# Gate rows of a mixture-of-experts layer spread over the partitions by DMA instead of by matmul

## The reference, cut to what matters

```
x = x + attention(ln_over_channels(x))        # per image, 256 tokens, one head
t = tokens of x                               # 1024 x 64
xt = ln(t)
probs = softmax(xt @ Wr + br)                 # 8 experts
top_p, top_idx = top_k(probs, 2)
weights = top_p / sum(top_p)                  # the two gates of a token
xn = ln(xt)
y[e] = gelu((xn * ln_g[e] + ln_b[e]) @ W1[e] + b1[e]) @ W2[e] + b2[e]     # 64 -> 256 -> 64
out = t + weights[0] * y[top_idx[0]] + weights[1] * y[top_idx[1]]
```

## Time and profile before

| | us |
|---|---|
| median of 3 runs | 68.73 (68.43 to 68.88) |
| time of the profiled execution | 68.35 |
| its span, first to last instruction | 66.6 |
| TensorE matmul busy | 60.2 (90% of the span) |
| VectorE busy | 38.2 (57%) |
| ScalarE busy | 33.9 (51%) |
| GpSimd busy | 27.6 (41%) |

### The profile page before, as it was taken

One profiled execution on the slowest core, in us unless ns is written; L12 is line 12 of the kernel. 1 busy time (PEld: TensorE's weight loads), 2 busy tenths in 40 slices (PEclk: granted clock), 3 DMA queues, 4 the chain that ended last, 5 costly groups with the idle time before them and its releaser, 6 DMA issues.

```text
span 66.6 us, 1224 instructions
## 1 busy us (share of the span) xinstructions
PE 60.2 (90%) x364; PEld 32.9 (49%) x364; DVE 38.2 (57%) x164; ACT 33.9 (51%) x78; POOL 27.6 (41%) x53
## 2 busy tenths in 40 slices
PE   2998799799799999999998799999999999999940
PEld 0315366588356687752765434435152644353630
DVE  2368699279995997931099924807040924049640
ACT  5301356832379995397479991770724392700000
POOL 5766880004599982360798000433443000705200
PEclk9999999999999999999999999999999999999999
DMA  0343478620000000000000000000000000000311
GB/s 0 96 94 57 152 167 253 262 110 5 0 0 0 15 0 0 0 0 0 5 0 0 10 0 0 0 0 0 0 0 0 0 0 0 0 0 0 89 40 43
DMA packets 2959, 2.33 MB, mean 35 GB/s; under 512 B 1924, under 2 KB 2568, under 8 KB 2952
## 3 DMA queue, kind: packets, MB, share of 16 engines
q1 hardware_dynamic: 2632, 2.21, 11.6%
q10 hardware_dynamic: 320, 0.03, 0.4%
HBM read 1.98 MB, written 0.26 MB: 34 GB/s over the span
## 4 chain that ended last, share of the span: by engine, by line
PE 62%; DVE 22%; issue 4%; DMA 4%; SPq 3%; ACT 2%; DVEq 0%
PE banks L927 22%; PE banks L891 21%; PE banks L848 4%; DMA X<-in_x_dram 4%; DVE nmax L519 3%; PE banks L911 3%; PE banks L833 3%; DVE KS L513 2%; DVE X L505 2%; PE banks L870 2%; SPq L256 2%; PE banks L944 2%; ACT PR L388 2%; DVE T L537 1%; DVE X L569 1%
## 5 line engine op out<-in xcount | busy, mean ns | idle before, releaser
L424 ACT ACTIVATE H<-banks,PF 128x512 f32<-128x512 f32 x32 | 20.4, 686 | 11.2 <-PE banks L891 10.8
L891 PE MATMUL banks<-XE,W1F 64*128 64x256 f32 x128 | 18.2, 402 | 0.2 <-ACT H L424 0.2
L927 PE MATMUL banks<-H,W2F 128*64 128x512 f32 x64 | 15.4, 603 | 0.0
L327 POOL TENSOR_TENSOR acc<-acc,gated 128x512 f32<-128x512 f32 x5 | 6.4, 1276 | 19.2 <-DVE gated L664 19.2
L891 PEld LDWEIGHTS banks<-XE,W1F 64*128 64x128 f32 x128 | 11.1, 186 | 6.0 <-issue 4.9
L648 DVE COPY GS<-banks 128x512 f32<-128x512 f32 x8 | 5.5, 685 | 7.1 <-PE banks L911 7.1
L308 POOL TENSOR_SCALAR XE<-XF,PF,LB 128x256 f32<-128x256 f32 x15 | 8.2, 563 | 2.5 <-ACT XF L405 2.5
L789 PE MATMUL banks<-zeros 128*128 128x512 f16 x23 | 8.0, 467 | 1.3 <-POOL zeros L330 1.3
L664 DVE SCALAR_TENSOR_TENSOR gated<-banks,B2T,GS 128x512 f32<-128x512 f32 (+1 forms) x7 | 4.6, 673 | 7.0 <-PE banks L927 6.8
L292 POOL TENSOR_TENSOR rs<-base,half 128x4 f32<-128x4 f32 x4 | 4.1, 1016 | 9.8 <-DVE base L562 9.8
L927 PEld LDWEIGHTS banks<-H,W2F 128*64 128x64 f32 x64 | 4.0, 136 | 6.7 <-issue 6.6
(11 more groups left out here) (87 smaller groups left out, 71.9 us busy)
## 6 DMA issues: line engine op xcount, KB each, us to landing
W1F<-in_w_dram SPq DMA_DIRECT2D x1, 768.0 KB, 6.0
W2F<-in_w_dram SPq DMA_DIRECT2D x1, 512.0 KB, 5.5
W1F<-in_w_dram SPq DMA_DIRECT2D x1, 256.0 KB, 3.2
out_dram<-res SPq DMA_DIRECT2D x4, 64.0 KB, 1.8
X<-in_x_dram SPq DMA_DIRECT2D x2, 64.0 KB, 1.9
X<-in_x_dram SPq DMA_DIRECT2D x1, 128.0 KB, 2.4
WQK<-in_attn_w_dram ACTq DMA_DIRECT2D x2, 16.0 KB, 2.1
WQK<-in_attn_w_dram SPq DMA_DIRECT2D x2, 8.0 KB, 2.0
```

The lines of the kernel that those rows point to most:

```text
L327: nc.gpsimd.tensor_tensor(acc[h][:, :], acc[h][:, :], gated[s % 2][:, :], ALU.add)\
L424: nc.scalar.activation(H[:, r, :].rearrange("p (t n) -> p t n", t=PT), ps_z[g // J % 2][:, :, PIX * j:PIX * j + PIX], ACT.Gelu, bias=PF[:, ...
L891: nc.tensor.matmul(ps_z[q % 2][:, k, PIX * j:PIX * j + PIX], W1F[rows, e, j, :], XE[h][rows, e, :], start=True, stop=True).then_inc(z_read ...
L927: mm = nc.tensor.matmul(ps_y[s % 2][C * k:C * k + C, :], W2F[:, u, :], H[:, (2 * J * s + J * k + j) % RING, :], start=(j == 0), stop=(j == ...
```

## The change

The gates are no longer cut into fp16 parts, no longer scaled, and no longer spread by TensorE. `turn_gates(h)` transposes the fp32 `gate[h]` directly, 4 matmuls with the 128 x 8 gate as the weights and the fp32 identity as the moving operand, into 8 partitions. ScalarE copies that to `gateT[h]`, 8 rows of 512 fp32 values. SyncE writes it to a DRAM scratch `gates_kept[h]` (16 KB), waits for that to land, and reads each of the 8 rows back into 64 partitions by a DMA with a broadcast source: 2 DMAs of 128 KB for each step s, into a tile `GS[s]` of its own. `weigh(s)` waits for `gates_in[s]`. Stages 11 and 12 of the route, `spread`, `keep_gates`, `select_rows`, the clearing of `gcut` and the fp16 identity go. The order on TensorE and VectorE is written anew around the gap, `fold_sum` and `finish(0)` stand one step earlier, and `add_up(6)` is cut into two pieces of 256 columns.

```diff
+        gates_kept = nc.dram_tensor("gates_kept", [HALVES, E, TOK], F32, kind="Internal").ap()
-        ps_gates = [banks[:, 5 - 2 * h, :] for h in range(HALVES)]
+        ps_gates = banks[0:E, 5, :]
-        gcut = both("gcut", [P, TILES, P], F16)
-        gateT = both("gateT", [P, TOK], F16)
+        gateT = both("gateT", [E, TOK])
-        GS = both("GS", [P, TOK])
+        GS = [sb(f"GS{s}", [P, TOK]) for s in range(STEPS)]
...
+            for s in range(STEPS):                                  # SyncE
+                h, p = s // PAIRS, s % PAIRS
+                if p == 0:
+                    sp.wait_ge(gateT_ready, h + 1)
+                    sp.dma_start(gates_kept[h, :, :], gateT[h][:, :]).then_inc(gates_out[h], 16)
+                    sp.wait_ge(gates_out[h], 16)
+                for k in range(2):
+                    sp.dma_start(GS[s][C * k:C * k + C, :], gates_kept[h, 2 * p + k, :].partition_broadcast(C))\
+                        .then_inc(gates_in[s], 16)
...
-                nc.gpsimd.tensor_tensor(acc[h][:, :], acc[h][:, :], gated[s % 2][:, :], ALU.add)\
-                    .then_inc(acc_ready, 1)
+                cuts = 2 if s == STEPS - 2 else 1
+                for k in range(cuts):
+                    cols = slice(TOK // cuts * k, TOK // cuts * (k + 1))
+                    nc.gpsimd.tensor_tensor(acc[h][:, cols], acc[h][:, cols], gated[s % 2][:, cols], ALU.add)\
+                        .then_inc(acc_ready, 1)
...
-            select_rows()                                           # GpSimd's order
...
-                elif stage == 11:
-                    nc.vector.tensor_copy(gcut[h][:, :, 0:E], gate[h][:, :, :]).then_inc(gcut_hi, 1)
-                elif stage == 12:
-                    nc.vector.tensor_tensor(gcut[h][:, :, E:KG], gate[h][:, :, :], gcut[h][:, :, 0:E],
-                                            ALU.subtract).then_inc(gcut_ready, 1)
-            def keep_gates(s):
-                dve.wait_ge(G_ps, 2 * (s + 1))
-                nc.vector.tensor_copy(GS[s % 2][:, :], ps_G).then_inc(gs_ready, 1)
             def weigh(s):
                 dve.wait_ge(y_ps, 2 * (s + 1))
-                dve.wait_ge(gs_ready, s + 1)
+                dve.wait_ge(gates_in[s], 32)
...
             def turn_gates(h):                                      # TensorE
-                pe.wait_ge(gcut_ready, h + 1)
+                pe.wait_ge(gate_ready, h + 1)
                 for t in range(TILES):
-                    last = nc.tensor.matmul(ps_gates[h][:, P * slot(t):P * slot(t) + P], gcut[h][:, t, :],
-                                            identh[:, :], start=True, stop=True)
+                    last = nc.tensor.matmul(ps_gates[:, P * slot(t):P * slot(t) + P], gate[h][:, t, :], ident[:, :],
+                                            start=True, stop=True)
-            def spread(s):
-                for k in range(2):
-                    nc.tensor.matmul(ps_G[C * k:C * k + C, :], sel[:, 2 * p + k, :], gateT[h][:, :],
-                                     start=True, stop=True).then_inc(G_ps, 1)
...
             layer1(5)                                               # TensorE's order
-            spread(0)
+            layer2(1)
```

More of the change, by code:

```diff
@@ L43 @@
 EPS_C, EPS_T = 1e-6, 1e-5
-SG = 2.0 ** 10
-SB = 2.0 ** 8
-KG = 2 * E
 WARM = 8
@@ L237, in build_block @@
         h_ready = sem("h_ready")
-        G_ps = sem("G_ps")
-        gs_ready = sem("gs_ready")
         y_ps = sem("y_ps")
+        gates_in = [sem(f"gates_in{s}") for s in range(STEPS)]
+        gates_out = [sem(f"gates_out{h}") for h in range(HALVES)]
         gated_ready = sem("gated_ready")
@@ L335, in _ @@
                                     base=0, pattern=[[-1, P]], channel_multiplier=1).then_inc(ident_ready, 1)
-            for h in range(HALVES):
-                nc.gpsimd.memset(gcut[h][:, :, :], 0.0).then_inc(gcut_clear, 1)
             first_pow(0)
@@ L416, in turn_gates @@
                 act.wait_ge(gates_ps, h + 1)
-                nc.scalar.copy(gateT[h][:, :], ps_gates[h]).then_inc(gateT_ready, 1)
+                nc.scalar.copy(gateT[h][:, :], ps_gates).then_inc(gateT_ready, 1)
             def gelu(g):
@@ L619, in route @@
                     for k in range(2):
-                        last = nc.vector.tensor_scalar(wab[h][:, k, :], th[h][:, :], (0.5 - k) * SG, 0.5 * SG,
+                        last = nc.vector.tensor_scalar(wab[h][:, k, :], th[h][:, :], 0.5 - k, 0.5,
                                                        ALU.mult, ALU.add)
@@ L762, in _ @@
             route(1, 7)
-            for stage in range(9, 13):
-                route(1, stage)
-            keep_gates(0)
+            route(1, 9)
+            route(1, 10)
             weigh(0)
-            keep_gates(1)
             weigh(1)
-            keep_gates(2)
             weigh(2)
-            keep_gates(3)
             weigh(3)
-            keep_gates(4)
             weigh(4)
-            keep_gates(5)
             weigh(5)
-            keep_gates(6)
+            finish(0)
             weigh(6)
-            keep_gates(7)
-            finish(0)
             weigh(7)
@@ L894, in turn_gates @@
             def turn_gates(h):
-                pe.wait_ge(identh_ready, 1)
-                pe.wait_ge(gcut_ready, h + 1)
+                pe.wait_ge(gate_ready, h + 1)
                 if h == 0:
                     pe.wait_ge(PT_odd, IMG + 1)
+                else:
+                    pe.wait_ge(gateT_ready, h)
                 for t in range(TILES):
-                    last = nc.tensor.matmul(ps_gates[h][:, P * slot(t):P * slot(t) + P], gcut[h][:, t, :],
-                                            identh[:, :], start=True, stop=True)
+                    last = nc.tensor.matmul(ps_gates[:, P * slot(t):P * slot(t) + P], gate[h][:, t, :], ident[:, :],
+                                            start=True, stop=True)
                 last.then_inc(gates_ps, 1)
-            def spread(s):
[L905 to L910, removed]
-                    nc.tensor.matmul(ps_G[C * k:C * k + C, :], sel[:, 2 * p + k, :], gateT[h][:, :],
-                                     start=True, stop=True).then_inc(G_ps, 1)
             def layer2(s):
@@ L941, in fold_sum @@
                 pe.wait_ge(acc_ready, PAIRS - 1)
-                pe.wait_ge(gateT_ready, HALVES)
+                pe.wait_ge(scaled_ready, HALVES)
                 for t in range(TILES):
@@ L1022, in _ @@
             turn_gates(1)
+            layer2(2)
             layer1(8)
-            layer2(1)
-            spread(1)
             layer1(9)
-            spread(2)
+            layer2(3)
             layer1(10)
-            layer2(2)
-            spread(3)
             layer1(11)
-            layer2(3)
+            layer2(4)
             layer1(12)
-            layer2(4)
-            spread(4)
             layer1(13)
-            spread(5)
+            layer2(5)
             layer1(14)
-            layer2(5)
             layer1(15)
+            fold_sum()
             layer2(6)
-            spread(6)
-            fold_sum()
-            spread(7)
             layer2(7)
```

28 lines of the change are left out of this document (2 added, 26 removed).

## The result

The changed kernel takes 65.78 us (65.66 to 66.00, 4 runs) against 68.58 us for the kernel before in the same comparison: ratio 0.959, 95% interval 0.954 to 0.964. The profiled execution took 65.81 us with a span of 64.0.

A forecast was written before the change was run, and what follows sets the result against it. TensorE was taken to bound the kernel, so savings there count one for one: -2.24 + 0.10 - 0.75 + 1.35 = -1.54 us, median 67.2 us. The 8-in-10 range was 66.0 to 68.3.

The forecast's parts named there:

- What bounds the kernel: Whole chain: TensorE bounds from before 20.36 to 62.10 us, except one break through VectorE, 33.13 to 37.32.
- Part 1: Spreads on TensorE: removing them saves 2.24 us; the last layer2, no longer overlapping a spread, costs 0.10 more.
- Part 2: Router break of half 1: layer2(1) fills it, so waits ahead of layer1(7) and turn_gates(1) go, -0.75 us.
- Part 3: turn_gates in fp32: each turn takes about 1.0 us instead of 0.33 and 0.32, adding 1.35 us.
- Rival A: turn_gates: the fp32 turn is as cheap as the transposes (0.44), sum -2.66, median 66.1 us; chance 0.08.
- Part 4: VectorE, ScalarE, GpSimd: their changes are worth nothing; TensorE needs 3.99 us a step, ScalarE 2.7.
- Part 5: Gates' DRAM round trip: all hidden; GS[0] complete at 34.1 us, with slack 4.9 us.
- rival B: Round trip: a slow DMA leg; 5.4 us gives a result within 1% of before, median 68.8; chance 0.05.
- C: Broadcast reads: one 2 KB DRAM row holds the rate down; 69.5 us at 70 GB/s, some 76 at 57; chance 0.05.
- D: Engines beside the DMA writes: matmuls or GpSimd and VectorE steps slow; 5% gives 67.9 us, 10% 68.6; chance 0.08.
- Part 6: Tail after layer2(7): 4.5 us as before; cutting add_up(6) in two avoids a 0.2 us delay of fold_even.
- The sum: Whole kernel: -1.54 us, layer2(7) ending at 60.6 instead of 62.10, span 65.06, median 67.2 us.

The follow-up runs named there:

- 64-row insert: Changed kernel with an fp16 matmul of 8 columns, weights of 64 rows, put between the two layer1 of four of the five pairs: 66.48 us, ratio 0.970.
- 128-row insert: Changed kernel with an fp16 matmul of 8 columns, weights of 128 rows, put between the two layer1 of four of the five pairs: 67.12 us, ratio 0.979.
- the kernel with five legs: Changed kernel with five more DRAM round legs per half between the gates' landing and the broadcast reads: 71.50 us profiled, 73.29 in the only other execution.
- the kernel with the pairs apart: Changed kernel reordered to three layer1 pairs instead of five, with layer2(6) and layer2(7) apart: 67.52 us, ratio 0.985.
- the kernel that reads twice: Changed kernel with every broadcast read issued a second time into an unused spare tile: 65.82 us.

## Why the prediction was wrong

- **What bounds the kernel**: right. TensorE carries the chain before and after.
- **Part 1 (the spreads, -2.24, and +0.10)**: the price read at each place is right, but what replaces a spread was taken as nothing. Where a spread stood between two `layer1` it cost its own 0.34 and kept them apart, 0.19 more; and the +0.10 was not there: `layer2(7)` behind `layer2(6)` takes 1.76 (3.63 - 1.87), as it did behind the spread (1.77). The reason given for the 1.77, an overlap with the spread in particular, was wrong: `spread` and `layer2` have tiles of one shape, 128 x 64, and either will do.
- **Part 2 (the break, -0.75)**: right; both waits are gone in the chain, and `turn_gates(1)` came at 38.72 (38.8 forecast).
- **Part 3 (the gates in fp32, +1.35)**: right, 0.97 for each forecast 1.0: +1.29. The stream rate of `layer2` (0.94) was nearest. The loads of 8 columns, nearly nothing in the prediction, took 85 to 90 ns each, against 138 to 144 for the 128 columns of the transposes. Rival A was wrong for this kernel; that its 66.1 us lie near the 65.78 measured is chance, since the turn did not take 0.44.
- **Part 4**: the step that failed is here, in the sentence that a step needs "1.06 + 1.06 + 1.87 = 3.99 us". It measured 1.93 + 1.87 = 3.80. The price of one `layer1` was read where each stood behind something of another shape, and carried to a place where two stand together. The mechanism of the forecast was whole; this one term was mis-sized, by 0.95 us in five pairs of `layer1` (one of them in the 1.06 + 1.06 of the break) and, in part 1, by 0.11 for the `layer2`. The kernel with the new order alone shows the pairs at 1.93 us without the rest of the change.
- **Part 5 (the round trip)**: right in kind. The write took 1.5 us (1.8 assumed), the reads 3.0 (2.4), `GS[0]` at 34.7 (34.1), slack 4.2 (4.9); `weigh(0)` started at 37.41 (37.4). The leg of 5.4 us in rival B gives the time of before; 5.0 would do for a result within 1% of it. Rivals B, C and D fell: the reads of one row into 64 partitions are issued and land at some 200 GB/s, above the 76 from which C decides.
- **Part 6 (the tail)**: 4.46 us (64.0 - 59.54) against 4.50; the cut of the add mattered less than I had it.
- **The sum**: -1.54 forecast, -2.67 measured over the same stretch, the difference made up as said above. The range ended at 66.0 because it was built from the price of the turn and from rivals, and all terms that were taken from the chain as they stood had no width.

What the trace of before showed and I passed over: that a spread between two `layer1` costs 0.34 and one behind a `layer2` 0.22, which I entered as two prices without asking what the 0.12 were; and that `attend` takes 0.85 us of the chain behind its own shape and 1.03 behind a `layer1`. Part 5 rests on the first of the two, and I did not compare them.

## What to carry to other kernels

Where TensorE bounds, the price of a group of matmuls depends on its neighbour: of two groups of one tile shape put side by side, the second is cheaper by about one weight load, here 0.19 us. Before an instruction is credited with what its removal frees, put the new order into the old kernel: here that alone gave some two thirds of the gain. And a transpose written as an fp32 matmul with the identity costs 0.97 us where the transpose form costs 0.53.

## What the runs showed of the hardware that was not expected

- In these traces the first weight load of a group starts ahead of its first matmul behind a group of the same tile shape (by 0.21 us with the 64-row insert, 0.11 for `attend`), and together with it behind another shape. Two groups of 64 x 128 tiles took 1.93 us side by side against 2.12 apart, with a 64-row insert 2.03, with a 128-row insert 2.23; `attend`, with 128 x 128 tiles, 0.85 against 1.03; the second of two `layer2`, with 128 x 64 tiles, 1.76 against 1.87.
- After TensorE had stood still for 3.90 us (the kernel with five legs), the granted clock read 0.5, its level of 1.2 GHz, in the two slices that follow, and the next `layer2` took 3.53 us instead of 1.87. In the kernel with the pairs apart, with waits of 0.62 and 0.45 us, it stayed at 1.00. So this late transfer cost its wait and 1.7 us on top.
- A DMA of 16 KB from 8 partitions to DRAM was complete 1.5 us after issue on an idle queue (2.5 in the kernel that reads twice, where reads were still in flight: issued at 41.46, the next issue at 43.93), and a leg back took 1.6 us; 128 KB read from one 2 KB row into 64 partitions 3.0 us, one issued every 0.62 us. The same rate for twice as long beside the matmuls changed nothing (65.82 against 65.78 us).
